# A transformer decoder layer on one NeuronCore: gates, experts and third norm on 28 tiles of 128 tokens, query and key stacks sent through DRAM

## What is computed

```python
x = _layernorm(x + _L0_attn_ref(x, L0_attn_W))                 # softmax(x x^T / 16), thresholded, times x
x = _layernorm(x + _L0_xattn_ref(x, ctx_1024, ctx_1024, mask, Wq, bq, Wk, bk, Wv, bv, Wo, bo))  # 16 heads of 16
x = _layernorm(x + _L0_ffn_ref(x, L0_ffn_Wr, L0_ffn_Wi, L0_ffn_Wo))      # best 2 of 8 experts
```

## Time and profile before

| | us |
|---|---|
| median of 3 runs | 811.33 (808.01 to 813.28) |
| the profiled execution | 814.44 |
| its span, from first to last instruction | 812.7 |
| granted TensorE clock, mean | 0.979 |

### The profile page before, as it was taken

The page is one execution under the profiler, slowest core; times in us unless marked ns, Lnnn a source line. Parts: engine busy times, 40 slices in busy tenths (PEclk is TensorE's granted clock), DMA queues, the critical chain, the costliest instruction groups (busy, mean ns, idle before and its releaser), DMA issues.

```text
span 812.7 us, 22214 instructions
## 1 busy us (share of the span) xinstructions
PE 768.0 (95%) x7288; PEld 663.1 (82%) x7288; DVE 694.0 (85%) x2649; ACT 594.1 (73%) x1449; POOL 205.2 (25%) x296
## 2 busy tenths in 40 slices
PE   5778899999999999999999999999999999999885
PEld 4667788888888888888888888888888888888663
DVE  4385799899999989999999999999989999998656
ACT  2246787778888778778878777777878787787660
POOL 4330222212232222212222222222232222222001
PEclk8898899999999999999999999999999999999999
DMA  7654344444444544444444444444445444443100
GB/s 221 168 134 123 97 121 111 121 114 121 110 122 119 129 119 113 112 117 123 120 116 122 119 118 109 122 119 117 119 117 125 122 115 116 117 117 87 46 12 12
DMA packets 91346, 92.69 MB, mean 114 GB/s; under 512 B 17040, under 2 KB 87072, under 8 KB 91232
## 3 DMA queue, kind: packets, MB, share of 16 engines
q1 hardware_dynamic: 91232, 91.28, 44.5%
HBM read 28.44 MB, written 3.90 MB: 40 GB/s over the span
## 4 chain that ended last, share of the span: by engine, by line
PE 50%; DVE 19%; SPq 15%; issue 11%; DMA 4%; ACT 1%; POOL 0%; DVEq 0%; POOLq 0%
PE psum L1106 8%; PE psum L1079 7%; PE psum L1280 7%; SPq L278 6%; SPq L287 6%; PE psum L1092 5%; DVE mix L929 4%; DVE scores_left L717 3%; PE psum L1176 3%; DMA x_sb<-in_x 3%; DVE x L812 3%; PE psum L1164 3%; PE psum L1152 2%; PE psum L1209 2%; PE psum L1187 2%
## 5 line engine op out<-in xcount | busy, mean ns | idle before, releaser
L717 DVE CUSTOM_DVE_ANT_0 scores_left<-psum,mask_add 112x375 f32<-112x375 f32 x512 | 272.3, 541 | 39.2 <-PE psum L1079 31.1
L483 ACT ACTIVATE probsT<-psum 125x448 f32<-125x448 f32 x384 | 199.5, 538 | 29.0 <-PE psum L1092 26.3
L468 ACT ACTIVATE psum<-mask_u 125x448 f32<-125x448 uint8 x384 | 205.9, 546 | 2.1
L1079 PE MATMUL psum<-k_stack,q_stack 96*112 96x376 f32 x512 | 185.4, 373 | 8.0 <-issue 3.9
L1092 PE MATMUL psum<-q_stack,k_stack 97*125 97x224 f32 x768 | 157.3, 287 | 2.3 <-ACT psum L468 2.0
L1092 PEld LDWEIGHTS psum<-q_stack,k_stack 97*125 97x125 f32 x768 | 132.6, 190 | 11.8 <-ACT psum L468 3.5
L929 DVE SCALAR_TENSOR_TENSOR mix<-psum,gate,mix 112x256 f32<-112x256 f32 x224 | 107.5, 480 | 8.0 <-PE psum L1280 3.0
L1280 PE MATMUL psum<-we_hi,x_hi 128*112 128x512 f32 x256 | 104.1, 406 | 1.0 <-DVE mix L929 1.0
L1079 PEld LDWEIGHTS psum<-k_stack,q_stack 96*112 96x112 f32 x512 | 91.6, 179 | 16.1 <-issue 8.1
L1280 PE MATMUL psum<-we_hi,x_lo 128*112 128x512 f32 x256 | 100.9, 394 | 0.0
L1280 PE MATMUL psum<-we_lo,x_hi 128*112 128x512 f32 x256 | 100.7, 393 | 0.0
(11 more groups left out here) (156 smaller groups left out, 1672.7 us busy)
## 6 DMA issues: line engine op xcount, KB each, us to landing
k_stack<-k_hi SPq DMA_DIRECT2D x256, 93.8 KB, 2.2
q_stack<-q_hi SPq DMA_DIRECT2D x256, 56.0 KB, 2.0
ctx_sb<-in_context_T SPq DMA_DIRECT2D x32, 376.0 KB, 3.6
k_stack<-k_lo SPq DMA_DIRECT2D x128, 93.8 KB, 2.2
q_stack<-q_lo SPq DMA_DIRECT2D x128, 56.0 KB, 2.0
xT<-in_x_T SPq DMA_DIRECT2D x32, 112.0 KB, 2.5
x_sb<-in_x SPq DMA_DIRECT2D x32, 112.0 KB, 3.4
out_dram<-out_sb SPq DMA_DIRECT2D x32, 112.0 KB, 2.7
```

The lines of the kernel that those rows point to most:

```text
L468: nc.scalar.activation(psum[0:KP, ST_BANKS[i % 2], 0:4 * TOK].rearrange("p (h q) -> p h q", h=4), mask_u8[b % MASKS][:, KEYS + t * TOK:KEY ...
L483: nc.scalar.activation(probsT[:, place, i % KT, :], psum[0:KP, ST_BANKS[i % 2], 0:4 * TOK], ACT.Exp, scale=-1.0).then_inc(probs_ready, 1)
L717: nc.vector.tensor_tensor_reduce(scores_left[:, n % 2, :], psum[0:TOK, S_BANKS[n % 2], 0:KEYS], mask_add[b % 2][:, :], 1.0, 3.0e38, ALU.ad ...
L1079: nc.tensor.matmul(psum[0:TOK, S_BANKS[n % 2], 0:KEYS_EVEN], q_stack[s][0:96, c, pair, odd, :], k_stack[s][0:96, c, pair, :], start=True, ...
```

## The change

**Tiles of 128 tokens.** 32 times 112 tokens are 28 times 128. The gates, experts and third norm (`lg`, `m0` to `m3`, `gate...`, `expert`, `stats3` to `out`, `store`) now run on tiles of 128 tokens that cross the batches. In an iteration whose batch number is a multiple of eight (0, 8, 16, 24) none of these steps is there: `at_tile` leaves them out. The transposed x2 goes into a ring of four tiles (`x2_high`, `x2_low`; `ring_parts`), in one or two pieces. The untransposed x2, to which `expert` adds, is put together by DMA: `move_head` and `move_tail` copy a batch's rows into `x2_tile`, and expert 0 waits for both. Widths in the free direction do not change: `m0` to `m3` are again six matmuls of 512 columns each, the operations of DVE again 256 or 8 elements long, now on 128 partitions.

**Stacks through DRAM.** `q_hi`, `q_lo`, `k_hi`, `k_lo` are written whole into `q_scratch` and `k_scratch` in DRAM, four DMAs, and read back into the stacks with one DMA for each third, six more. A reading DMA waits for the writing one. `scores(b, 0)` waits for all six; scores 1 to 3 wait for none. The row of maxima goes from `nmaxT` straight into the stack.

**Orders.** The lists of all five engines are new. `m3` and the transposes `x1T` and `x2T` move across the border into the next iteration, and gates and experts are otherwise as many iterations behind as before. On PE the key projection `K0` of the next batch comes right behind scores 7, and between it and scores 0 of that batch stand eight blocks (8 to 11 and 0 to 3), eight scores (8 to 15), `V0`, `V2`, `V1` (L1187 to L1209 before), both halves of `weigh_values`, `m0`, `m1`, and the small steps `mx0`, `PT`, `att`, `oT`, `aT`, `Wo`, `mx1`. Between scores 0 and the next `K0` stand `m2`, `m3`, `x1T`, `x2T`, `qT`, `Sc`, `lg`, `K1`, four blocks and scores 1 to 7. On ACT `k_hi0` comes behind exponent 8, and `nmaxT0` behind it. The weights of experts 5 to 7 are loaded one after the other into the place of expert 0, the products of the experts (`E4` to `E7`) come an iteration later, and the loads of batch 1 come ahead of the experts' weights. On POOL `fill_ones` and `low_context` of batch 0 come ahead of `var1` and `rstd1` of batch 0.

The diff, cut to what the text speaks of:

```diff
+ROWS = 128
+STEP = ROWS - TOK
+SPAN = TOK // STEP + 1
+TILES = BATCH * TOK // ROWS
+RING_TILES = 4
+TILE_BUFFERS = 3
+TILE_STEPS = ("lg", "m0", "m1", "m2", "m3")
...
+    return 0 <= b < BATCH and (name not in TILE_STEPS or b % SPAN > 0)
+
+
+def tile_of(b):
+
+    return b - b // SPAN - 1
+
...
+def ring_parts(b):
+
+    at = TOK * b % (RING_TILES * ROWS)
+    first = min(TOK, RING_TILES * ROWS - at)
+    return [(0, first, at)] + ([(first, TOK, 0)] if first < TOK else [])
+
+
+def overwritten_by(b):
+
+    return (TOK * (b + 1) - 1) // ROWS - RING_TILES + 1
 
 
...
+        late = sb("late", [128, 6 * DIM])
+        out_sb = [late[:, k * DIM:(k + 1) * DIM] for k in range(2)]
+        mix = late[:, 2 * DIM:3 * DIM]
+        x2_tile = [late[:, k * DIM:(k + 1) * DIM] for k in (4, 5, 3)]
...
+            def move_head(b):
+
+                rows = STEP * (b % SPAN)
+                if rows > 0:
+                    sp.wait_ge(done["x2"], b + 1)
+                    sp.dma_start(x2_tile[tile_of(b) % TILE_BUFFERS][ROWS - rows:ROWS, :], x2[b % 2][0:rows, :])\
+                      .then_inc(head_in[tile_of(b) % TILE_BUFFERS], 16)
...
+            def write(scratch, part, written, b):
+                sp.dma_start(scratch, part.bitcast(fp32)).then_inc(written[b % 2], 16)
...
+            def low_keys_out(b):
+                sp.wait_ge(done["k_lo0"], b + 1)
+                settle(sp)
+                write(k_scratch[b % 2][1], k_lo[:, :, :].rearrange("p c k -> p (c k)"), k_lo_out, b)
...
+            def stack_keys(b, third):
+
+                if third == 0:
+                    sp.wait_ge(k_hi_out[b % 2], turn(b, 1, 2))
+                    settle(sp)
+                if third == 1:
+                    sp.wait_ge(k_lo_out[b % 2], turn(b, 1, 2))
+                    settle(sp)
+                sp.dma_start(k_stack[b % STACKS][32 * third:32 * third + 32, :, :, :]
+                             .rearrange("p n c k -> p n (c k)").bitcast(fp32),
+                             k_scratch[b % 2][(0, 1, 0)[third]].rearrange("(n p) x -> p n x", n=PAIRS))\
+                  .then_inc(k_stacked[b % STACKS], 16)
...
+                if c == 0:
+                    sp.wait_ge(done["nmaxT0"], b + 1)
+                    settle(sp)
+                if c == 1:
+                    sp.wait_ge(done["nmaxT1"], b + 1)
+                    settle(sp)
+                sp.dma_start(q_stack[b % STACKS][96:97, :, :, c, :].rearrange("o p h q -> o (p h) q").bitcast(fp32),
+                             nmaxT[c][:, :].bitcast(fp32)).then_inc(neg_max_in[b % STACKS][c], 16)
...
+                at(it + 1, high_keys_out)
+                at(it, neg_max_to_stack, 0)
+                at(it + 1, low_keys_out)
+                at(it + 1, stack_queries, 2)
+                at(it + 1, stack_queries, 1)
+                at(it + 1, stack_queries, 0)
+                at(it + 1, stack_keys, 0)
+                at(it - 2, move_head)
+                at(it + 1, stack_keys, 2)
+                at(it + 1, stack_keys, 1)
+                if it + 3 > 1:
+                    at(it + 3, load_context)
+                if it + 3 > 1:
+                    at(it + 3, load_x)
+                at(it, neg_max_to_stack, 1)
                 if it == 0:
...
+                at(it - 4, rstd2)
+                at_tile(it - 5, var3)
+                at(it - 1, mask)
+                at(it - 2, x1_bo)
+                at_tile(it - 5, rstd3)
...
+                if n == 0:
+                    pe.wait_ge(q_stacked[s], turn(b, 3, STACKS))
+                    pe.wait_ge(k_stacked[s], turn(b, 3, STACKS))
...
-            def mix_experts(b, name):
-
-                free(name, b)
-                hi, lo = x2_high[b % 2], x2_low[b % 2]
+            def mix_experts(t, name):
+
+                free(name, batch_of(t))
+                in_ring = slice(t % RING_TILES * ROWS, (t % RING_TILES + 1) * ROWS)
+                hi, lo = x2_high[:, :, in_ring], x2_low[:, :, in_ring]
...
```

More of the change, by code:

```diff
@@ L209, in decoder_layer @@
         wk_sb = place(probsT_all, 6)
-        early = [(place(wout_sb, 2 * e), place(wout_sb, 2 * e + 1)) for e in range(2)]
-        early += [(place(probsT_all, 2 * e), place(probsT_all, 2 * e + 1)) for e in range(3)]
-        wi_wout = early + [early[0], early[1], early[0]]
-        EARLY, FORMER = 5, {5: 0, 6: 1, 7: 5}
+        v_last = v_sb[STACKS - 1][:, :, :, :].rearrange("p t h d -> p (t h d)")
+        own = [(place(late, 0), place(late, 1)), (place(late, 2), place(v_last, 0))]
+        own += [(place(probsT_all, 2 * e), place(probsT_all, 2 * e + 1)) for e in range(3)]
+        wi_wout = own + [own[0]] * 3
+        EARLY, FORMER = 5, {5: 0, 6: 5, 7: 6}
         def expert_slot(e):
-            return e if e < EARLY else (e - EARLY) % 2
+            return e if e < EARLY else 0
         banks = dict(zip(("G0", "G1", "G2"), G_BANKS))
@@ L251, in at, with at_tile @@
                 step(b, *which)
+        def at_tile(b, step, *which):
+            if live(b) and b % SPAN > 0:
+                step(tile_of(b), *which)
         block = ctx.enter_context(nc.Block())
@@ L662, in _ @@
             for k in range(STACKS):
-                nc.vector.memset(v_sb[k][:, :, :, HEAD_DIM:HEAD_DIM + 1], 1.0)
-                nc.vector.memset(k_stack[k][0:96, :, :, KEYS:KEYS_EVEN].bitcast(fp32), 0.0)
+                if k < STACKS - 1:
+                    nc.vector.memset(v_sb[k][:, :, :, HEAD_DIM:HEAD_DIM + 1], 1.0)
+            for part in (k_hi, k_lo):
+                nc.vector.memset(part[:, :, KEYS:KEYS_EVEN].bitcast(fp32), 0.0)
             nc.vector.memset(o_bank[:, 0:GROUPS * TOK], 0.0)
@@ L1247, in expert_product @@
             def expert_product(e):
-                pe.wait_ge(expert_in[expert_slot(e)], 32 * (1 + len([n for n in range(EARLY, e + 1) if expert_slot(n) == expert_slot(e)])))
+                pe.wait_ge(expert_in[expert_slot(e)], 32 * (e - EARLY + 2 if e >= EARLY else 1))
                 free(f"E{e}", 0)
```

753 lines of the change are left out of this document (386 added, 367 removed), and 21 rows, old and new, of tables (STEPS, USES).

## The result

| us | before | after |
|---|---|---|
| median | 809.67 (806.17 to 813.28) | 897.76 (894.45 to 908.65) |
| ratio | | 1.107 (95%: 1.100 to 1.115) |
| span of the profiled execution | 812.7 | 894.2 |
| granted clock, mean | 0.979 | 0.942 |

The forecast was 791 us, its range 770 to 824. One of the four executions after, that of 908.65 us, was in a slower state of the chip, and the ratio is taken without it. In the profile after, the second norm's line is 925, x2T 1263, scores 1198, V1 1319, K0 1286, the experts' matmuls 1403, and DVE's `expert` is 1047.

What follows compares the result with a forecast made beforehand. The prediction took PE, busy 99% of the steady stretch, as the bound. Full iterations -6, light ones -14, start +2 and end -2 summed to -20 us: 791 us against the median, range 770 to 824.

Steps and rivals of the forecast that it cites:

- Stacks through DRAM: SP's queue relieved, 10 starts for 24; keys before scores 0 land 0.3 us late in a full iteration, between 0 and 1.5.
- the 12.6 us that the keys take: From K0's end to keys landed: 2.7 + 1.8 us plus 2.22 MB, 11.4 to 13.8 us, middle taken.
- The last rival: Keys at the narrow rate: transfers into 32 partitions under 200 GB/s, keys after 15.5 us, 870 us; chance 0.06.
- What PE gives: PE's work from the end of K0 to scores 0: 12.3 us, in a light iteration 9.5.
- The small steps some 1.4 (an estimate): PE's small steps between K0's end and scores 0, put at 1.4 us of the 12.3.
- 0 to -0.75 us for each: Gain in each of 25 full iterations from new POOL orders and fewer waits; -0.55 taken before the keys are counted.
- The waits of 12.9 and 8.9 us: PE's idle in the old kernel: x2T waiting 12.9 us for the second norm, 8.9 us for loads of x.
- The lateness rival: Keys late at 240 GB/s: 13.8 us, 1.5 over, all iterations wait at scores 0; 821 us; chance 0.15.
- x2 by DMA, cost 0: Two more transfers per batch and expert 0's wait cost nothing; at most 2 us an iteration if SP's queue delays them.
- The second norm: DVE's second norm, held by POOL's ctx_lo, should take 0.4 us instead of 1.235, ending x2T's wait.
- Light iterations bound by keys: Iterations without gates and experts take 19.4 us: keys' 12.6 plus 6.8 of PE's list; 4 x -3.5 = -14 us.
- What would show it: Signs listed beforehand; wrong if scores 0 waits above 1 us everywhere, clock below 1.00 mid-kernel, or light iterations over 21 us.

Runs made afterwards that it cites:

- the third: On the kernel with loads in the idle stretch and early x2 head copy (865.7 us), queries neither written nor read back from the fourth batch on: 809.14 us.
- the seventh experiment: Each stack read cut in two, scores 0 awaiting first halves only: changed kernel 812.41 us; with loads in the gap, early head and early first norm 792.79 us.
- the second kernel of 2.: Changed kernel with loads of x and context moved into the idle DMA stretch and x2's head copied ahead of the high keys' write: 865.67 us.
- that of 4.: On the kernel at 865.7 us, POOL's rows of ones moved behind the root of batch 0's first norm: 859.45 us.
- first experiment: Changed kernel with pieces moved ahead of the high keys' write: x2 head copy 897.05 us, query reads 920.11, loads 929.37, all three 954.86.
- the mixed one: On the kernel at 859.5 us, queries go straight from SBUF into the stack in 12 transfers, only keys through DRAM: 909.96 us.

## Why the prediction was wrong, step by step

**The step that failed** is "*Stacks through DRAM*", and in it the 12.6 us that the keys take: "0.3 us late in a full iteration, between 0 and 1.5". In the changed kernel they took 16.5 in the iteration shown, and scores 0 came 16.0 us after K0's end on the average of the full ones. Its parts:

- The rate. I took the middle of 240 and 321 GB/s; reads into the stacks run at 221 with the engines full. 240 had been scaled up from a half-filled window of direct transfers, and 321 is that of loads into 128 partitions. The last rival came nearest, with 870 us for 898, and I gave it 0.06. Its "under 200 GB/s" is still too low, and its mechanism is not quite what the rows show: the 16 engines are filled (1.03), and move 221 GB/s all the same. The measured 221 lies near the 218 GB/s that the Trainium skill, page "SBUF — State Buffer", section "Door 1: The DMA port swizzle (why [64,N] ≈ [32,N])", gives as the limit for eight ports, above its 189 for 1 MiB; and 223 against 355 to 380 agrees with its port table, by which 0 to 63 reach eight of the ports and 32 to 95 all of them. With the measured 221 the sum would have been 2.7 + 1.8 + 10.0 = 14.5 us.
- The bytes. I counted 2.22 MB, what is written and read from k_lo on. Between the start of k_hi's write (410.58) and the landing (425.62) the engines moved 15.0 us x 226 GB/s = 3.4 MB: to the 2.22 come the write of k_hi, the copy of x2 and most of 0.6 MB of context and x, which the diff starts right behind the last read and the text did not count. Moving the loads was worth 31 us, 27 of them in the steady stretch: some 13 by the clock (an estimate, half of the 27 us that it no longer stands at the lower level), the rest since the last read lands 0.7 us sooner. With loads and copy away, 15.0 us are left.
- The time from K0's end until SP writes k_lo, 3.0 us, was right (2.7).

**What PE gives** was too short as well, 12.3 us for a measured 13.83, which worked the other way. "The small steps some 1.4 (an estimate)" are 2.0, since Wo alone takes 1.05, and the passages from one kind of step to the next take 0.05 to 0.1 us more than starts within a kind. The new order also has a wait of its own that the sum did not name: ahead of scores 15 PE waits some 0.4 us for DVE's maximum of the score before, in nearly every iteration (`PE psum L1198 <- DVE nmax L832: 11.5, 28, 0.9`), in the kernels of the third and the seventh experiment too. So a full iteration without any wait for keys is 23.38 us, not 22.2; "0 to -0.75 us for each" was a gain that is not there. The waits of 12.9 and 8.9 us on which it rested were read too high: each adds the idle time of PE and that of its weight loads, which overlap. By PE's starts in the kernel before, x2T came 0.2 us late in most iterations and the loads of x cost 2.6 us in the steady stretch, together about 9 us of 666, or 0.3 an iteration. And PE's list is itself longer in the new order.

**The price of a wait.** The lateness rival named the point (0.75 us) and the half clock "if each wait did that, 25 x 1.1 more", and gave 821 or, with that, 848. In the changed kernel a full iteration is made up of 23.4 us of PE's list and 2.0 us of waits at V1 and scores 0: 25.4. The half clock comes on top in 13 of the 28 iterations from batch 4 on, and costs 1.2 to 1.4 us where it lasts 3.4: 26.7. Most full iterations measure 25 to 27.5. Together the clock stands at its lower level for 72 of the 749.6 us. In the second kernel of 2., where V1 does not wait, it fell behind five waits at scores 0, of 1.8 to 3.6 us, and not behind the others, of 0.1 to 1.6 us; in that of 4. it stayed up behind one of 1.8. So what the rival said of each wait holds for about every second iteration.

**x2 by DMA, cost 0:** wrong for the order as it stands. The copy queues behind four reads, expert 0 waits for it, and V1 behind that; the chain gives 15% to it. But it hid a wait that was due anyway (first experiment), so its own price in time was nil.

**What was right.** The second norm takes 0.404 us for 1.235, so POOL's `ctx_lo` was what held it, and x2T's wait went. SP's queue is 8% of the chain, for 15% before. The 16 more rows cost nothing (six matmuls 1.40 us). Light iterations bound by keys: forecast 19.4 with 12.6 us of keys; with 16 they measured 22.3 to 23, and 19.0 where the keys are in time, near ACT's 17.2. The start was +3.6 us (forecast +2, for the reason given: PE waited 11.5 us for x1 of batch 0), the end -5.3 (forecast -2).

The list "What would show it" had the signs of this outcome: clock below 1.00, waits of 1 us at scores 0 in every iteration, light ones over 21.

## What to carry to other kernels

When transfers are gathered into fewer and larger ones behind one wait, the wait moves from the first piece to the last. Sum all that the queue holds from the first start to the last landing, other traffic too, and let the consumer wait by halves: here this one cut was worth some 83 us and saved no byte. An idle DMA window a few us away is the place for loads that nobody is waiting for; moving a transfer forward in a queue that is already backed up only puts it ahead of something more urgent. And a forecast within 0.3 us of a threshold that every iteration crosses is no forecast: the bounds of the slowest term belong in the chances.

## What the runs showed of the hardware that I had not expected

- A small transfer in a backed-up queue waits its turn: 3.5 KB behind 1.6 MB held PE up to 4.3 us.
- A DMA whose outer dimension is 4 keeps 0.28 of the engines busy and moves 93 GB/s.
- A stretch of queries with a read into partitions 32 to 95 ran at 355 to 380 GB/s, the stretch of keys behind it, into 64 to 95 and 0 to 63, at 223. I tried no kernel in which all stack reads cover both sets; whether it would beat 792.8 us is open, since there the keys are in time already.
- SP's start of one transfer takes 0.32 to 0.7 us by shape, at times more with a full queue: the three reads of queries took 1.3 to 2.1 us in the changed kernel, the three reads of keys 1.4 to 2.9 in the mixed one.
- In the iteration shown of the changed kernel two waits of 1.2 us within 3 us were followed by half clock, in that of the second kernel of 2. a single one of 1.0 us was not; over the kernels the length of a wait alone does not tell which it will be.
